# Cross-attention pair on one core: the layer norm's doubling moved into gamma, the second queries summed half by half, the scores begun on the first half of the queries

## The chip, the cores and the metric

The kernel runs on one core of a Trainium2 chip, as a single program with one instruction stream for each engine: TensorE (PE; the loading of its weights is shown as PEld), VectorE (DVE), ScalarE (ACT), GpSimd (POOL) and SyncE (SP). The metric is the device time of one launch in microseconds (us), as the median of several runs.

## What is computed

Sixteen blocks of 512 tokens with 256 features (`x`, 16 x 512 x 256) pass through two cross-attentions onto 64 context rows per block. The part of the reference that the change touches is the second one:

```python
q = gelu(einsum('bqd,dp->bqp', virtual_node, Wq) + bq)     # virtual_node is x', what the first attention gives
k = gelu(einsum('bnd,dp->bnp', node_features, Wk) + bk)
v = gelu(einsum('bnd,dp->bnp', node_features, Wv) + bv)
scores = einsum('bqp,bnp->bqn', q, k)
attended = einsum('bqn,bnp->bqp', softmax(scores), v)
x = einsum('bqp,pd->bqd', attended, Wf) + bf + virtual_node
mu = mean(x); var = mean((x - mu)^2)
return (x - mu) * rsqrt(var + 1e-5) * ln_gamma + ln_beta
```

The first attention normalises tokens and context by their root mean square, lets each token attend to the context row that its index names and to that row's two neighbours, with 16 heads and squared-relu weights, projects and adds the tokens.

## The kernel before

All of it works on features by tokens: a block is a tile of 128 partitions by 2 halves of the features (`c` or `g`, 0 and 1) by 512 tokens. The loop `steps` runs over 17 steps; step s works on five blocks at once: e = s (loading), a = s-1 (first queries and key products), f = s-2 (first attention's values), b = s-3 (first output projection, x', second queries and scores) and n = s-4 (softmax, output, layer norm, write). The last block is finished after the loop by code of its own, in halves of the tokens (names with `half_`). Every engine has its instructions in the order in which the program writes them, and semaphores (`wait_ge`, `then_inc`) tie the engines together; no planner orders anything. A product in full precision is three matmuls (`product`, L430 to L434): the high part of weight and data, low weight with high data, high weight with low data. So each operand is split in a rounded high part and a remainder.

The places that the change and the prediction speak of, within one step:

- **x' and its split.** DVE adds projection and tokens into `xpT`, second half of the features first (L1100). ACT rounds each half into `xp_hi` (L896), DVE takes the remainder `xp_lo` of each half (L1103), also second half first.
- **The second queries.** `queries1(0)` and `queries1(1)` on PE (L627 to L642) each sum six matmuls over both halves of x', c = 0 first. Ahead of `queries1(0)` PE waits until both halves of `xp_hi` and of `xp_lo` are there. Between the two stands `up_keys(a)` (L638, matmuls of L479), which writes the PSUM banks from which the layer norm reads, and so waits for `zn_ready`, which ACT raises after the last of the four scalings of block n.
- **Gelu and scores.** ACT makes `q1T` from the two results (L909) and raises `q1_ready` once, after both. PE's scores (L662) wait for that.
- **The layer norm.** PE's output matmuls of block n (L590) are followed by DVE's statistics (L1089, four instructions), ten small POOL instructions on 128 x 4 values (`norm_factors`, L351 to L372), ACT's four scalings to `zn` (L862, in two pairs with a copy of L829 between them), POOL's product with gamma (L381) and sum with beta (L383), and the write. POOL's factors: `half_rstd` is half of 1/std (L368, a power), `rstd` doubles it (L371), `nbias` is minus the mean over the std (L372), from `nmean2` (L366).
- **On POOL behind gamma and beta** stands the remainder of the next tokens, `x_lo` (L343), for which PE's first queries wait.

The functions that the diff touches follow with their line numbers.

Of the kernel before, what the change touches and what calls it, by code (L numbers as in the profile page):

```python
# [23 lines left out]
def xattn_pair(nc: bass.Bass, xT, ctx, ctxT, idx, vectors, wq0T, wk0T, wv0T, wo0T,  # L24
# [9 lines left out]
    with es:  # L34
# [3 lines left out]
        def sem(name):  # L38
            return es.enter_context(nc.semaphore(name))
# [10 lines left out]
        lnb_row = sb("lnb_row", [P, D])  # L50
        minus_half = sb("minus_half", [P, CT])
# [53 lines left out]
        def rows(t):  # L105
# [46 lines left out]
            "stats_ready", "parts_ready", "gap_ready", "mean_ready", "var_ready", "rstd_ready", "nbias_ready"))  # L152
        kvs_zero = [sem(f"kvs_zero_{r}") for r in range(2)]
# [166 lines left out]
        def _(pool):  # L320
# [30 lines left out]
            def norm_factors(n):  # L351
# [14 lines left out]
                G.tensor_scalar(nmean2[:, :], mean2[:, :], -1.0, None, ALU.mult).then_inc(mean_ready, 1)  # L366
# [4 lines left out]
                G.tensor_tensor(rstd[:, :], half_rstd[:, :], half_rstd[:, :], ALU.add).then_inc(nbias_ready, 1)  # L371
                G.tensor_tensor(nbias[:, :], nmean2[:, :], half_rstd[:, :], ALU.mult).then_inc(nbias_ready, 1)  # L372

            def scale_rows(n):

                pool.wait_ge(zn_ready, 2 * n + 2)
                if n == 0:
                    pool.wait_ge(ln_in, 16 * 2)
                else:
                    pool.wait_ge(out_done, 16 * n)  # L380
                G.tensor_tensor(zo, zn, lng_row[:, :].unsqueeze(1).broadcast_to([P, TT, D]), ALU.mult).then_inc(zg_ready, 1)  # L381
                pool.wait_ge(zg_ready, n + 1)
                G.tensor_tensor(zo, zo, lnb_row[:, :].unsqueeze(1).broadcast_to([P, TT, D]), ALU.add).then_inc(zo_ready, 1)  # L383
# [6 lines left out]
            def step(e, a, f, b, n):  # L390
                if n is not None:
                    norm_factors(n)
                    scale_rows(n)
                if e is not None:
                    split_x_lo(e)
                if n is not None:
                    write_rows(n)
# [12 lines left out]
            scale_rows(LAST - 1)  # L410
# [7 lines left out]
        def _(pe):  # L418
# [133 lines left out]
            def step(e, a, f, b, n):  # L552
# [74 lines left out]
                def queries1(i):  # L627
                    for c in range(DC):
                        product(ps[:, Q1_BANKS[i], :], *weight("q1", c, i), xp_hi[:, c, :], xp_lo[:, c, :], c == 0, c == DC - 1, q1_mm)

                if b is not None:
                    pe.wait_ge(xph_ready, 2 * b + 2)
                    pe.wait_ge(xpl_ready, 2 * b + 2)
                    queries1(0)
# [22 lines left out]
                if b is not None:  # L657
                    pe.wait_ge(q1_ready, b + 1)

                    for c in range(DC):  # L660
                        for h in range(2):
                            i = mm(ps[h * K:(h + 1) * K, 4, 0:2 * P], k1T[:, c, b * K:(b + 1) * K],  # L662
                                   q1T[:, c, 2 * h * P:(2 * h + 2) * P], start=(c == 0), stop=(c == DC - 1))
# [109 lines left out]
        def _(act):  # L773
# [81 lines left out]
            def step(e, a, f, b, n):  # L855
                def normalise(tiles):

                    act.wait_ge(nbias_ready, 2 * n + 2)
                    if n > 0:
                        act.wait_ge(zg_ready, n)  # L860
                    for j in tiles:
                        i = A(zn[:, j, :], out_rows(j), ACT.Identity,  # L862
                              bias=nbias[:, j:j + 1], scale=rstd[:, j:j + 1])
                    i.then_inc(zn_ready, 1)
# [41 lines left out]
                if b is not None:  # L906
                    for i in range(DC):
                        act.wait_ge(q1_mm, 2 * b + i + 1)
                        last = A(q1T[:, i, :], ps[:, Q1_BANKS[i], :], ACT.Gelu, bias=vec[:, 2, i:i + 1])  # L909
                    last.then_inc(q1_ready, 1)  # L910
# [344 lines left out]
```

## Time and profile before

| | us |
|---|---|
| median of 3 runs | 372.47 |
| lowest and highest run | 370.99, 372.87 |
| the profiled execution's own time | 372.61 |
| its span, first to last instruction | 370.8 |
| PE busy, DVE busy, ACT busy, POOL busy in the span | 338.5, 311.5, 246.6, 180.4 |

The profile shows one execution. Busy time is the time in which an engine has an instruction in work; idle time is given with what ended it. The page also follows the chain of work back from the last instruction, at each step to what released it. Matmuls overlap each other in the records, so that what counts on PE is the distance from one start to the next, not the duration.

### The profile page before, as it was taken

To read this page: it belongs to the slowest core of one execution; us is meant where nothing else is said; L and a number is where in the kernel's file an instruction comes from. 1 tells how busy PE (TensorE), PEld (TensorE's weight loads), DVE (VectorE), ACT (ScalarE), POOL (GpSimd) and SP (SyncE) were. 2 spreads that over 40 slices of the span, in tenths; PEclk is the share of its full clock that TensorE was granted. 3 is DMA by queue.
4 is the path that set the end of the run, shared out by engine and by line. 5 is a ranking of instruction groups with operands and counts; after the bars stand their busy time and mean duration, and the time that the engine had idled before them with its cause. 6 is when DMAs were issued, how large, how long until landed. Compare 5 with 4: busy or idle time off the path is not lost.

```text
span 370.8 us, 5551 instructions
## 1 busy us (share of the span) xinstructions
PE 338.5 (91%) x1904; PEld 238.5 (64%) x1904; DVE 311.5 (84%) x486; ACT 246.6 (66%) x491; POOL 180.4 (49%) x218
## 2 busy tenths in 40 slices
PE   3995899999999999999999999999999999986871
PEld 1571486767676767676767686858686767655740
DVE  0878588699999999999999999999989898986745
ACT  4796243275959595959595959595959595847552
POOL 3712210023838383838383737474747474626063
PEclk9997899999999999999999999999999999999995
DMA  7978211931222222323231313141414131010103
GB/s 245 319 228 236 74 57 40 216 113 54 91 103 95 98 100 91 109 85 114 75 124 60 138 60 139 60 139 59 141 57 142 57 143 57 2 57 0 58 0 113
DMA packets 21946, 38.48 MB, mean 104 GB/s; under 512 B 2144, under 2 KB 8288, under 8 KB 21920
## 3 DMA queue, kind: packets, MB, share of 16 engines
q1 hardware_dynamic: 18800, 29.48, 24.9%
q0 software_dynamic: 2160, 7.87, 6.1%
q10 hardware_dynamic: 960, 0.79, 0.7%
q8 instruction: 15, 0.25, 0.3%
q14 instruction: 11, 0.09, 0.1%
HBM read 17.29 MB, written 8.39 MB: 69 GB/s over the span
## 4 chain that ended last, share of the span: by engine, by line
PE 56%; ACT 12%; POOL 11%; DVE 11%; issue 10%; ACTq 0%; POOLq 0%
PE ps L510 8%; ACT bufs L862 6%; PE ps L432 6%; PE ps L434 6%; PE ps L433 6%; PE ps L479 5%; DVE stats L1089 5%; PE ps L662 4%; PE ps L561 4%; PE ps L671 4%; PE ps L590 4%; PE ps L485 3%; POOL rstd L371 3%; PE ps L566 2%; ACT bufs L829 2%
## 5 line engine op out<-in xcount | busy, mean ns | idle before, releaser
L343 POOL TENSOR_TENSOR x_lo<-x_ring,x_hi 128x1024 fp32r<-128x1024 f32 x16 | 38.3, 2396 | 43.7 <-ACT x_hi L825 43.7
L1020 DVE TENSOR_TENSOR qkp<-ps,bufs 128x1024 f32<-128x1024 f32 x48 | 55.9, 1214 | 0.9 <-PE ps L479 0.8
L381 POOL TENSOR_TENSOR bufs<-bufs,lng_row 128x1024 f32<-128x1024 f32 x15 | 36.0, 2403 | 37.0 <-ACT bufs L862 35.0
L896 ACT ACTIVATE xp_hi<-bufs 128x512 fp32r<-128x512 f32 x30 | 18.9, 632 | 50.6 <-DVE bufs L1100 50.6
L1031 DVE TENSOR_TENSOR ps<-ps,wn 128x1024 f32<-128x1024 f32 x32 | 39.2, 1224 | 1.2 <-PE ps L485 1.2
L355 POOL TENSOR_TENSOR mean_gap<-stats 128x4 f32<-128x4 f32 x14 | 2.8, 197 | 71.1 <-DVE stats L1089 71.1
L383 POOL TENSOR_TENSOR bufs<-bufs,lnb_row 128x1024 f32<-128x1024 f32 x15 | 35.6, 2377 | 1.2
L510 PE MATMUL ps<-qkp,cst 128*32 128x512 f32 x192 | 32.2, 624 | 1.7 <-DVE qkp L1020 1.7
L510 PE MATMUL ps<-bufs,cst 128*32 128x512 f32 x64 | 31.9, 624 | 0.0
L862 ACT ACTIVATE bufs<-ps,nbias,rstd 128x256 f32<-128x256 f32 x56 | 28.6, 569 | 3.0 <-POOL nbias L372 3.0
L432 PE MATMUL ps<-xp_hi,wh_q 128*128 128x512 f32 (+1 forms) x68 | 27.1, 398 | 2.6 <-DVE xp_lo L1103 1.9
L829 ACT ACTIVATE bufs<-ps 128x512 f32<-128x512 f32 x32 | 19.0, 597 | 14.3 <-PE ps L434 14.3
L432 PE MATMUL ps<-x_hi,wh_q 128*128 128x512 f32 x64 | 26.5, 414 | 0.0
L432 PE MATMUL ps<-o_hi,wh_o 128*128 128x512 f32 (+1 forms) x68 | 26.0, 382 | 0.3 <-DVE o_lo L1172 0.3
L434 PE MATMUL ps<-xp_lo,wh_q 128*128 128x512 f32 (+1 forms) x68 | 25.8, 380 | 0.0
L433 PE MATMUL ps<-o_hi,wl_o 128*128 128x512 f32 (+1 forms) x68 | 25.8, 379 | 0.0
L433 PE MATMUL ps<-xp_hi,wl_q 128*128 128x512 f32 (+1 forms) x68 | 25.8, 379 | 0.0
L434 PE MATMUL ps<-o_lo,wh_o 128*128 128x512 f32 (+1 forms) x68 | 25.6, 377 | 0.0
L434 PE MATMUL ps<-x_lo,wh_q 128*128 128x512 f32 x64 | 25.1, 393 | 0.0
L433 PE MATMUL ps<-x_hi,wl_q 128*128 128x512 f32 x64 | 25.1, 391 | 0.0
L909 ACT ACTIVATE bufs<-ps,vec 128x512 f32<-128x512 f32 x30 | 20.6, 689 | 5.3 <-PE ps L434 5.2
L1100 DVE TENSOR_TENSOR bufs<-ps,x_ring 128x512 f32<-128x512 f32 x30 | 20.5, 685 | 4.2 <-PE ps L434 4.1
(205 smaller groups left out, 924.4 us busy)
## 6 DMA issues: line engine op xcount, KB each, us to landing
x_ring<-xT SPq DMA_DIRECT2D x16, 512.0 KB, 3.5
out<-bufs POOLq DMA_DIRECT2D x15, 512.0 KB, 3.4
idx_ring<-idx SPq DMA_DIRECT2D x16, 256.0 KB, 4.1
kvs<-kv SPq DMA_DIRECT2D x32, 126.0 KB
wkv_lo<-kv SPq DMA_DIRECT2D x32, 126.0 KB
vfd<-bufs SPq DMA_DIRECT2D x8, 256.0 KB, 4.1
qkp<-ctxT SPq DMA_DIRECT2D x2, 512.0 KB, 7.2
bufs<-ctx SPq DMA_DIRECT2D x2, 512.0 KB, 8.5
```

The lines of the kernel that those rows point to most:

```text
L343: G.tensor_tensor(x_lo[:, :, :], x_ring[:, e % RING, :, :], f32_view(x_hi[:, :, :]), ALU.subtract).then_inc(xl_ready, 2)
L381: G.tensor_tensor(zo, zn, lng_row[:, :].unsqueeze(1).broadcast_to([P, TT, D]), ALU.mult).then_inc(zg_ready, 1)
L383: G.tensor_tensor(zo, zo, lnb_row[:, :].unsqueeze(1).broadcast_to([P, TT, D]), ALU.add).then_inc(zo_ready, 1)
L432: mm(o, hi, m_hi, start=start, stop=False)
L433: mm(o, lo, m_hi, start=False, stop=False)
L434: last = mm(o, hi, m_lo, start=False, stop=stop)
L510: i = mm(ps[32 * s:32 * s + 32, 0, :], sum_sel[:, g if s < SHIFTS else 2, :], qk[:, s, g, :] if s < SHIFTS else xsq[:, g, :], start=(g == ...
L829: A(q0[:, g, :], ps[:, Q0_BANKS[g], :], ACT.Copy).then_inc(q0_cp, 1)
L862: i = A(zn[:, j, :], out_rows(j), ACT.Identity, bias=nbias[:, j:j + 1], scale=rstd[:, j:j + 1])
L909: last = A(q1T[:, i, :], ps[:, Q1_BANKS[i], :], ACT.Gelu, bias=vec[:, 2, i:i + 1])
L1020: V.tensor_tensor(qk[:, s, :, :], ps[:, bank0:bank0 + 2, :], q0, ALU.mult).then_inc(qk_ready, 1)
L1031: V.tensor_tensor(dst.rearrange("p a (h d) -> p (a h) d", d=HD), picked(bank0).rearrange("p a (h d) -> p (a h) d", d=HD), wn[:, s, :, :].r ...
```

## The change

Three edits. First, `queries1` takes c = 1 ahead of c = 0, and the two waits for `xp_hi` and `xp_lo` are split: `queries1(0)` waits for the second half only, and for the first half when it comes to it. Second, ACT raises `q1_ready` after each gelu, and PE waits ahead of each half of the scores' sum for its own half of the queries; the halves stay in their order. Third, L371 (`rstd`) is dropped from `norm_factors`: ACT scales by `half_rstd`, `nmean2` is made with -0.5 in the place of -1.0, so that `zn` is half of what it was, and POOL multiplies by `lng_twice`, which is twice gamma and made once, at block 0. The last block's own code keeps gamma and `rstd`.

```diff
@@ -48,6 +48,7 @@
         bf_row = sb("bf_row", [P, D])
         lng_row = sb("lng_row", [P, D])
         lnb_row = sb("lnb_row", [P, D])
+        lng_twice = sb("lng_twice", [P, D])
         minus_half = sb("minus_half", [P, CT])
         x_ring = sb("x_ring", [P, RING, DC, T])
         idx_ring = sb("idx_ring", [P, RING, T], i32)
@@ -150,6 +151,7 @@
         eT_mm, eT_ready, z_mm = map(sem, ("eT_mm", "eT_ready", "z_mm"))
         stats_ready, parts_ready, gap_ready, mean_ready, var_ready, rstd_ready, nbias_ready = map(sem, (
             "stats_ready", "parts_ready", "gap_ready", "mean_ready", "var_ready", "rstd_ready", "nbias_ready"))
+        twice_ready = sem("twice_ready")
         kvs_zero = [sem(f"kvs_zero_{r}") for r in range(2)]
         kvs_in = [sem(f"kvs_in_{r}") for r in range(2)]
         zn_ready, zg_ready, zo_ready, out_done, last_zg, last_zo, last_out_done = map(sem, (
@@ -363,22 +365,23 @@
                 pool.wait_ge(var_ready, 2 * n + 1)
                 G.tensor_tensor(var4[:, :], m2_part[:, :], gap_sq[:, :], ALU.add).then_inc(var_ready, 1)
                 pool.wait_ge(mean_ready, 2 * n + 1)
-                G.tensor_scalar(nmean2[:, :], mean2[:, :], -1.0, None, ALU.mult).then_inc(mean_ready, 1)
+                G.tensor_scalar(nmean2[:, :], mean2[:, :], -0.5, None, ALU.mult).then_inc(mean_ready, 1)
                 pool.wait_ge(var_ready, 2 * n + 2)
                 G.tensor_tensor(half_rstd[:, :], var4[:, :], minus_half[:, 0:TT], ALU.pow).then_inc(rstd_ready, 1)
                 pool.wait_ge(rstd_ready, n + 1)
                 pool.wait_ge(mean_ready, 2 * n + 2)
-                G.tensor_tensor(rstd[:, :], half_rstd[:, :], half_rstd[:, :], ALU.add).then_inc(nbias_ready, 1)
                 G.tensor_tensor(nbias[:, :], nmean2[:, :], half_rstd[:, :], ALU.mult).then_inc(nbias_ready, 1)
 
-            def scale_rows(n):
+            def scale_rows(n, gamma):
 
                 pool.wait_ge(zn_ready, 2 * n + 2)
                 if n == 0:
                     pool.wait_ge(ln_in, 16 * 2)
+                    G.tensor_tensor(lng_twice[:, :], lng_row[:, :], lng_row[:, :], ALU.add).then_inc(twice_ready, 1)
+                    pool.wait_ge(twice_ready, 1)
                 else:
                     pool.wait_ge(out_done, 16 * n)
-                G.tensor_tensor(zo, zn, lng_row[:, :].unsqueeze(1).broadcast_to([P, TT, D]), ALU.mult).then_inc(zg_ready, 1)
+                G.tensor_tensor(zo, zn, gamma[:, :].unsqueeze(1).broadcast_to([P, TT, D]), ALU.mult).then_inc(zg_ready, 1)
                 pool.wait_ge(zg_ready, n + 1)
                 G.tensor_tensor(zo, zo, lnb_row[:, :].unsqueeze(1).broadcast_to([P, TT, D]), ALU.add).then_inc(zo_ready, 1)
 
@@ -390,7 +393,7 @@
             def step(e, a, f, b, n):
                 if n is not None:
                     norm_factors(n)
-                    scale_rows(n)
+                    scale_rows(n, lng_twice)
                 if e is not None:
                     split_x_lo(e)
                 if n is not None:
@@ -407,7 +410,7 @@
                 G.tensor_tensor(nbias[:, cols], mean2[:, cols], rstd[:, cols], ALU.mult).then_inc(half_nbias, 1)
 
             norm_scales(0, slice(0, TT))
-            scale_rows(LAST - 1)
+            scale_rows(LAST - 1, lng_row)
             norm_scales(1, slice(0, 2))
             norm_scales(2, slice(2, TT))
             write_rows(LAST - 1)
@@ -625,12 +628,14 @@
                     centre_keys(a)
 
                 def queries1(i):
-                    for c in range(DC):
-                        product(ps[:, Q1_BANKS[i], :], *weight("q1", c, i), xp_hi[:, c, :], xp_lo[:, c, :], c == 0, c == DC - 1, q1_mm)
+
+                    for c in (1, 0):
+                        if i == 0:
+                            pe.wait_ge(xph_ready, 2 * b + (2 - c))
+                            pe.wait_ge(xpl_ready, 2 * b + (2 - c))
+                        product(ps[:, Q1_BANKS[i], :], *weight("q1", c, i), xp_hi[:, c, :], xp_lo[:, c, :], c == 1, c == 0, q1_mm)
 
                 if b is not None:
-                    pe.wait_ge(xph_ready, 2 * b + 2)
-                    pe.wait_ge(xpl_ready, 2 * b + 2)
                     queries1(0)
                 if a is not None:
                     if n is not None:
@@ -655,9 +660,8 @@
                 if f == 0:
                     final_values(1)
                 if b is not None:
-                    pe.wait_ge(q1_ready, b + 1)
-
                     for c in range(DC):
+                        pe.wait_ge(q1_ready, 2 * b + c + 1)
                         for h in range(2):
                             i = mm(ps[h * K:(h + 1) * K, 4, 0:2 * P], k1T[:, c, b * K:(b + 1) * K],
                                    q1T[:, c, 2 * h * P:(2 * h + 2) * P], start=(c == 0), stop=(c == DC - 1))
@@ -855,12 +859,12 @@
             def step(e, a, f, b, n):
                 def normalise(tiles):
 
-                    act.wait_ge(nbias_ready, 2 * n + 2)
+                    act.wait_ge(nbias_ready, n + 1)
                     if n > 0:
                         act.wait_ge(zg_ready, n)
                     for j in tiles:
                         i = A(zn[:, j, :], out_rows(j), ACT.Identity,
-                              bias=nbias[:, j:j + 1], scale=rstd[:, j:j + 1])
+                              bias=nbias[:, j:j + 1], scale=half_rstd[:, j:j + 1])
                     i.then_inc(zn_ready, 1)
 
                 if n is not None:
@@ -906,8 +910,7 @@
                 if b is not None:
                     for i in range(DC):
                         act.wait_ge(q1_mm, 2 * b + i + 1)
-                        last = A(q1T[:, i, :], ps[:, Q1_BANKS[i], :], ACT.Gelu, bias=vec[:, 2, i:i + 1])
-                    last.then_inc(q1_ready, 1)
+                        A(q1T[:, i, :], ps[:, Q1_BANKS[i], :], ACT.Gelu, bias=vec[:, 2, i:i + 1]).then_inc(q1_ready, 1)
                 if e is not None:
                     split_x_hi(e)
                 if b is not None:
```

What it does to the instructions of POOL in `norm_factors`. Before (from the variance, in every step with a block n; at block 0 here):

```order
L366 TENSOR_SCALAR nmean<-mean 128x4 [waits mean_ready]
L368 TENSOR_TENSOR half_rstd<-var,minus_half 128x4 [waits var_ready]
L371 TENSOR_TENSOR rstd<-half_rstd 128x4 [waits mean_ready,rstd_ready]
L372 TENSOR_TENSOR nbias<-nmean,half_rstd 128x4
L381 TENSOR_TENSOR bufs<-bufs,lng_row 128x1024 [waits ln_in,zn_ready]
L383 TENSOR_TENSOR bufs<-bufs,lnb_row 128x1024 [waits zg_ready]
```

Of the change, at the same place:

```order
L368 TENSOR_SCALAR nmean<-mean 128x4 [waits mean_ready]
L370 TENSOR_TENSOR half_rstd<-var,minus_half 128x4 [waits var_ready]
L373 TENSOR_TENSOR nbias<-nmean,half_rstd 128x4 [waits mean_ready,rstd_ready]
L380 TENSOR_TENSOR lng_twice<-lng_row 128x256 [waits ln_in,zn_ready]
L384 TENSOR_TENSOR bufs<-bufs,lng_twice 128x1024 [waits twice_ready]
L386 TENSOR_TENSOR bufs<-bufs,lnb_row 128x1024 [waits zg_ready]
```

One instruction is gone and `nbias` stands in its place, with its waits; the doubling of gamma is there at block 0 alone.

PE at the end of the loop, step 17, where no block a is left: the second queries up to the back-transposes of x' (L671 before, L675 now). Before:

```order
L432 MATMUL ps<-xp_hi,wh_q 128x512
L433 MATMUL ps<-xp_hi,wl_q 128x512
L434 MATMUL ps<-xp_lo,wh_q 128x512
L485 MATMUL ps<-kv,onehot 128x256 [waits xp_ready]
L485 MATMUL ps<-kv,onehot 128x256 x3
L662 MATMUL ps<-bufs,k1T 64x256 [waits q1_ready]
L662 MATMUL ps<-bufs,k1T 64x256 x3
L671 MATMUL ps<-cst,bufs 128x128 [waits zn_ready]
```

Of the change:

```order
L435 MATMUL ps<-xp_hi,wh_q 128x512 [waits xpl_ready,xph_ready,att_ready]
L436 MATMUL ps<-xp_hi,wl_q 128x512
L437 MATMUL ps<-xp_lo,wh_q 128x512
L435 MATMUL ps<-xp_hi,wh_q 128x512 [waits xpl_ready,xph_ready]
...
L488 MATMUL ps<-kv,onehot 128x256 [waits xp_ready]
L488 MATMUL ps<-kv,onehot 128x256 x3
L666 MATMUL ps<-bufs,k1T 64x256 [waits q1_ready]
L666 MATMUL ps<-bufs,k1T 64x256
L666 MATMUL ps<-bufs,k1T 64x256 [waits q1_ready]
L666 MATMUL ps<-bufs,k1T 64x256
L675 MATMUL ps<-cst,bufs 128x128 [waits zn_ready]
```

The matmuls are the same in number and size; a second pair of waits stands in the middle of the first queries' sum and a second wait in the middle of the scores' sum.

## Rows read from the trace of the kernel before

**Rows 1.** The page: busy time, its share of the span and the instructions of each engine

```profile
PE 338.5 (91%) x1904; PEld 238.5 (64%) x1904; DVE 311.5 (84%) x486; ACT 246.6 (66%) x491; POOL 180.4 (49%) x218
```

**Rows 2.** The chain of waits from 195 to 240 us, one block: start, us, what

```profile
202.32 0.75 POOL rstd L371
...
205.73 0.74 PE ps L479 x2
...
224.48 0.73 PE ps L479 x2
```

**Rows 3.** L371's duration (ns, min/median/max), and one of the waits

```profile
L371 POOL TENSOR_TENSOR rstd<-half_rstd x14: 200/747/757, 89.9 to 333.3; 128x4 f32<-128x4 f32 x14
...
ACT bufs L862 <- POOL nbias L372: 3.0, 13, 0.8
```

**Rows 4.** Timeline, 202.2 to 203.3 us: start, duration, engine, line, operation, [idle before]

```profile
202.32 0.75 POOL L371 TENSOR_TENSOR rstd<-half_rstd 128x4 f32<-128x4 f32 x1
202.32 1.47 DVE L1103 TENSOR_TENSOR xp_lo<-bufs,xp_hi 128x512 fp32r<-128x512 f32 x2
202.44 0.63 ACT L896 ACTIVATE xp_hi<-bufs 128x512 fp32r<-128x512 f32 x1 [0.32 <-DVE bufs L1100]
...
203.02 0.20 POOL L372 TENSOR_TENSOR nbias<-nmean,half_rstd 128x4 f32<-128x4 f32 x1
...
203.25 0.56 ACT L862 ACTIVATE bufs<-ps,nbias,rstd 128x256 f32<-128x256 f32 x1 [0.18 <-POOL nbias L372]
```

**Rows 5.** Timeline of block 0, 89.8 to 90.7 us

```profile
89.86 0.20 POOL L371 TENSOR_TENSOR rstd<-half_rstd 128x4 f32<-128x4 f32 x1
...
90.01 0.65 POOL L372 TENSOR_TENSOR nbias<-nmean,half_rstd 128x4 f32<-128x4 f32 x1
```

**Rows 6.** Timeline of PE from 203.3 to 206.3 us

```profile
203.38 0.61 PE L479 MATMUL ps<-onehot,kv 128*128 128x512 f32 x2
203.94 0.47 PE L432 MATMUL ps<-xp_hi,wh_q 128*128 128x512 f32 x1
...
205.18 0.40 PE L434 MATMUL ps<-xp_lo,wh_q 128*128 128x512 f32 x1
```

**Rows 7.** Timeline of PE, ACT and DVE, 207.4 to 211.2 us

```profile
207.68 0.62 PE L479 MATMUL ps<-onehot,wkv_lo 128*128 128x512 f32 x2
...
207.88 0.69 ACT L909 ACTIVATE bufs<-ps,vec 128x512 f32<-128x512 f32 x1 [0.21 <-PE ps L434]
...
208.14 0.63 PE L485 MATMUL ps<-kv,onehot 128*128 128x256 f32 x4
...
208.70 1.08 PE L662 MATMUL ps<-bufs,k1T 128*64 128x256 f32 x8
...
211.06 0.42 DVE L1129 TENSOR_REDUCE nmax<-ps 128x4 f32<-128x256 f32 x1 [0.33 <-PE ps L675]
```

**Rows 8.** Timeline of POOL, block 0, and of PE where it needs x_lo

```profile
98.02 2.38 POOL L343 TENSOR_TENSOR x_lo<-x_ring,x_hi 128x1024 fp32r<-128x1024 f32 x1
...
101.75 0.47 PE L432 MATMUL ps<-x_hi,wh_q 128*128 128x512 f32 x1
```

**Rows 9.** Timeline of step 17, the last of the loop, 332 to 341.5 us

```profile
333.35 0.59 POOL L371 TENSOR_TENSOR rstd<-half_rstd 128x4 f32<-128x4 f32 x1
333.89 0.65 POOL L372 TENSOR_TENSOR nbias<-nmean,half_rstd 128x4 f32<-128x4 f32 x1
...
334.57 1.94 ACT L862 ACTIVATE bufs<-ps,nbias,rstd 128x256 f32<-128x256 f32 x4 [0.82 <-POOL nbias L372]
...
337.82 1.27 ACT L909 ACTIVATE bufs<-ps,vec 128x512 f32<-128x512 f32 x2
...
339.14 1.08 PE L662 MATMUL ps<-bufs,k1T 128*64 128x256 f32 x8 [1.06 <-ACT bufs L909]
```

**Rows 10.** Stretches: us, busy PE, PEld, DVE, ACT, POOL, granted clock, DMA

```profile
345.00:353.00 8.00, 7.32 (x57) 6.41 (x56) 4.88 (x15) 3.74 (x6) 1.03 (x1) 1.00 0.01 2
...
361.00:363.00 2.00, 1.62 (x5) 0.70 (x3) 1.77 (x9) 0.00 (x0) 0.38 (x1) 0.50 0.00 0
```

## The prediction, made before the changed kernel ran

> **What bounds the kernel now.** I read the page first: PE has work in 91% of the span, DVE in 84% [rows 1]. So no engine is free to take much, and the question for each edit is which wait ends last where it acts. The chain of waits answers for the middle of the run [rows 2]. It repeats every 18.75 us (205.73 to 224.48), and always in the same way: PE's output matmuls of block n, DVE's statistics, POOL's small instructions, ACT's scalings, and PE's `up_keys` (L479), which must not write the banks before the last scaling has read them. From there PE runs through to the next output matmuls. So the layer norm of block n is on the path, and the POOL instruction that the change drops, L371, is a link of it with 0.75 us. The durations come from one execution with 372.61 us of its own; the median of the runs is 372.47, so 0.14 comes off the sum at the end.
>
> **The layer norm's doubling.** L371 takes 0.75 us in nearly every block, at least 0.20 [rows 3]. At block 6 it starts at 202.32 with DVE's first remainder (L1103) and ends at 203.07; L372 ends at 203.22 and ACT starts scaling at 203.25, after 0.18 of idle time [rows 4]. Block 0 shows what the 0.75 is: there L371 came through in 0.20 just ahead of L1103, and L372 took 0.65 in its place [rows 5]. Two instructions of the same kind and size; whichever stands beside DVE's first remainder is held until that is over. L371 has no work worth 0.75, and `nbias`, which moves into its place, will be held in the same way. Were the 0.75 work, `nbias` would end so early that ACT alone set the start, 0.28 sooner in each block, and the sum would be that of rival 1. The Trainium skill, "SBUF — State Buffer", section "Who interferes with whom", speaks against this part of the change: a VectorE instruction with two SBUF inputs, as L1103 is, and a GpSimd one that reads SBUF exclude each other for the whole instruction, and the first to issue wins. The rows of blocks 0 and 6 agree: a held instruction ends when the first remainder does.
>
> So `nbias` will end at 203.07 instead of 203.22: 0.15 earlier. ACT can take it: its previous instruction (L896) ends at 202.44 + 0.63 = 203.07, and back to back ACT overlaps two such instructions by 0.10 (four scalings of 0.56 in 1.94, rows 9). ACT's idle time before scaling adds up to 3.0 us over 13 blocks, 0.8 of it at the last [rows 3]: 2.2 over 12, 0.18 each, so the twelve blocks are alike. **12 x 0.15 = 1.8 us.** Block 0 had next to no idle time there; between 0.03 and 0.16, I take 0.1. The bounds for each of the twelve are 0 (something else holds `up_keys`) and 0.18 + 0.10 = 0.28 (`nbias` is early and ACT itself is the limit).
>
> Do the others follow a step that is 0.15 shorter? PE has 0.32 to spare ahead of `up_keys`: its last query matmul started at 205.18, they follow one another every 0.23, and L479 started at 205.73 [rows 2, 6]. DVE idles 0.33 before the maxima of the scores, for PE [rows 7], and everything else before them on DVE is further ahead of its users. So both have slack for 0.15, and DVE would be the next bound at 0.33.
>
> **The second queries' order.** `queries1(0)` now waits for both halves of the remainder: it starts at 203.94 instead of 203.38 + 2 x 0.23 = 203.84 [rows 6], 0.15 after L1103's second half (203.79, rows 4). With c = 1 first it need not wait, which gives back 0.10 and some 0.09 of a slower first matmul. But behind it stands `up_keys`, where PE already has 0.32 too many, and the gain lies in that wait. I take 0 in the twelve blocks; if the wait there went away it would be worth 0.19. Step 3, which has no layer norm, could gain those 0.19 once; I leave them out. An order of 1, 0 costs nothing in itself: the same six matmuls. POOL's, SP's and ACT's queues are not reordered.
>
> **The scores' first half.** In the middle of the run PE reaches L662 at 208.70, 0.13 after the second gelu's end at 208.57 [rows 7]. In step 17, where PE really stood waiting for gelu, it started 0.05 after its end (337.82 + 1.27 = 339.09, rows 9). So in the middle PE does not wait, and the term is 0; at most 0.08 a block. The added waits, when already satisfied, cost nothing: L485 at 208.14 has one ahead of it and follows the second matmul of L479 (207.68 + 0.23 = 207.91) after the usual 0.23 [rows 7]. The upper end for one is the 0.19 of a wait that does stop PE.
>
> **Gamma doubled at block 0.** One POOL instruction of 128 x 256, about a quarter of L381's or L343's 2.4 us: 0.6 once. POOL's `x_lo` would end near 98.02 + 2.38 + 0.6 = 101.0, PE asks for it at 101.75 [rows 8]. Hidden; if that 0.75 were gone it would cost 0.6 once.
>
> **The end of the loop.** Step 17 has no block a and is bound otherwise: POOL, four scalings, a table load, two gelus, scores, each waiting for the one before [rows 9]. Here L372 was held by the second remainder too, and ACT idled 0.82 before scaling. Without L371 `nbias` is done when the first remainder is, at 333.35 + 0.59 = 333.94 instead of 334.54: 0.60 off. Then the first gelu ends near 337.9 and the second at 338.49, and PE sums the first half in between. The second half starts at 338.54 and takes half of 1.08, so the scores end at 339.1 to 339.2 instead of 340.22. PE is there in time: its queries can start on the first remainder too, 0.6 earlier. **1.05 us**, with bounds of 0.6 (the split brings nothing) and 1.4 (`nbias` is not held). What follows, the maxima and the last block's own code, waits for these scores and moves with them.
>
> **Sum:** 1.8 + 0.1 + 1.05 = 2.95; 372.61 - 2.95 = 369.66, and against the median 369.5.
>
> **Rivals.** (1) `nbias` slips through. In the middle blocks L371 and L1103 start at the same hundredth; at block 0 0.02 decided the other way. By the stamps POOL is not behind DVE there, so a shift of 0.02 could let `nbias` (0.20) through in every block. (The Trainium skill's "SBUF — State Buffer", section "Who interferes with whom", gives the lock to the first to issue, which by these stamps would be POOL.) Then ACT is the limit: 12 x 0.28 + 0.1 + 1.4 = 4.9, which gives 367.6. Against it: the stamps were as good as equal in all those blocks too, and POOL lost. Chance 0.17. (2) The middle gains nothing, because a wait that I read as slack takes the place of `nbias` (DVE before the maxima is the nearest, 0.33), or the blocks' gain is lost again on PE's added waits; only the end brings 1.05: 371.4. Chance 0.17. (3) Slower: PE's clock. It was granted in full up to 361 and at half, 1.2 GHz, behind it [rows 10], after PE had stood waiting for the softmax of the last block. The change moves the waits of the end against that grant. If it fell before 345, the 7.3 us of PE's busy time in the stretch to 353 would double, and the last block's code is a chain in which little else could cover it: up to 369.5 + 7.3 = 376.8. It decides if the grant is 0.50 anywhere in 341 to 353. Against it: PE stood still there before as well, and kept its clock. Chance 0.05. That the edit does not do what it says is part of the forecast: `nbias` inherits the stall, and the new order of the queries is hidden.
>
> **Chances and range.** The forecast has 0.56, (1) 0.17, (2) 0.17, (3) 0.05, and 0.05 is left for the rest. A measurement here can tell about 0.5% from no change, 1.86 us, so faster means below 370.6. The forecast and (1) are there, 0.73, and a little of the rest; (2) with most of the rest makes no change, 0.21; slower 0.05. The range takes in (1) and (2) with the runs' own scatter of some tenths: 367.4 to 371.6.
>
> **What would show it.** After the change: the distance from one `up_keys` to the next at 18.60 instead of 18.75; `nbias` with a duration near 0.75 and ACT's idle time before scaling near zero; PE's wait before the first second-query matmul gone and its wait for the scaling still there, longer by some 0.04; L662 in the middle no closer to the matmul before it; in step 17 the scores in two parts and the end of them 1.05 earlier against the statistics of that step. `nbias` at 0.20 and a distance of 18.47 would show (1); 18.75 again would show (2) and make me wrong, as would a step 17 that gains less than 0.6.

## The result, and the profile after

| | before | after |
|---|---|---|
| median of 11 runs each, us | 372.28 | 369.13 |
| lowest and highest | 370.54, 372.87 | 366.17, 370.94 |
| ratio, with its 95% interval | | 0.9932 [0.9909, 0.9955] |
| the profiled execution's own time, us | 372.61 | 369.03 |
| its span, us | 370.8 | 367.2 |

The kernel became faster by 0.7%, or 3.15 us between the medians; 2.95 were forecast (369.5). The interval of the ratio reaches from 0.45% to 0.91% faster. So a gain is clear of the noise, and the 0.5% that the prediction took as the least that a measurement can tell lies inside it: more than 0.5% is likely, not certain.

Block 6 of the changed kernel, its timeline where the rows of before are [rows 4, 6]: start, duration, engine, line, operation, and in brackets idle time and what ended it. L373 was L372, L1106 was L1103, L900 was L896, L866 was L862, L435 and L482 were L432 and L479.

```profile
200.63 1.48 DVE L1106 TENSOR_TENSOR xp_lo<-bufs,xp_hi 128x512 fp32r<-128x512 f32 x2
200.63 0.74 POOL L373 TENSOR_TENSOR nbias<-nmean,half_rstd 128x4 f32<-128x4 f32 x1
200.75 0.63 ACT L900 ACTIVATE xp_hi<-bufs 128x512 fp32r<-128x512 f32 x1 [0.32 <-DVE bufs L1103]
201.41 0.56 ACT L866 ACTIVATE bufs<-ps,nbias,half_rstd 128x256 f32<-128x256 f32 x1
201.68 0.61 PE L482 MATMUL ps<-onehot,kv 128*128 128x512 f32 x2
202.13 0.39 PE L435 MATMUL ps<-xp_hi,wh_q 128*128 128x512 f32 x1
203.27 0.39 PE L437 MATMUL ps<-xp_lo,wh_q 128*128 128x512 f32 x1
203.88 0.50 PE L482 MATMUL ps<-onehot,wkv_lo 128*128 128x512 f32 x1 [0.23 <-ACT bufs L866]
```

In this block, as in most, `nbias` has taken L371's place beside DVE's first remainder, and L371's duration. ACT now scales right after its rounding of x' ends (200.75 + 0.63 = 201.38). The second queries start 0.23 after the matmul before them (201.68 + 0.23 + 0.23 = 202.14, and the row has 202.13), without a wait, and PE waits as before at `up_keys`: 203.88 - 203.27 - 0.23 = 0.38, where it was 0.32.

The chain of waits of the changed kernel, from one block to the next (start, us, what), answers to [rows 2]:

```profile
200.63 0.75 POOL nbias L373
201.41 0.49 ACT bufs L866
...
203.88 0.73 PE ps L482 x2
...
222.48 0.73 PE ps L482 x2
```

The distance is 222.48 - 203.88 = 18.60; before it was 18.75. The duration of `nbias` over its 14 calls (ns: min, median, max) answers to [rows 3]:

```profile
L373 POOL TENSOR_TENSOR nbias<-nmean,half_rstd x14: 201/743/758, 89.2 to 330.6; 128x4 f32<-128x4 f32 x14
```

and from the list of waits (us in total, times, longest):

```profile
ACT bufs L866 <- POOL nbias L373: 0.2, 1, 0.2
```

ACT's idle time before scaling fell from 3.0 us to 0.2, and what is left is in step 17. That step's timeline, which answers to [rows 9]:

```profile
330.60 0.59 POOL L373 TENSOR_TENSOR nbias<-nmean,half_rstd 128x4 f32<-128x4 f32 x1
331.22 1.94 ACT L866 ACTIVATE bufs<-ps,nbias,half_rstd 128x256 f32<-128x256 f32 x4 [0.22 <-POOL nbias L373]
334.47 1.27 ACT L913 ACTIVATE bufs<-ps,vec 128x512 f32<-128x512 f32 x2
335.21 1.23 PE L666 MATMUL ps<-bufs,k1T 128*64 128x256 f32 x8 [0.48 <-ACT bufs L913]
```

The scores (L666) begin before the second gelu has ended (334.47 + 1.27 = 335.74), and end at 335.21 + 1.23 = 336.44. Counted from the start of the first remainder of x' in this step (330.44) that is 6.00; before it was 340.22 - 333.18 = 7.04.

**Where the 3.6 us between the two profiled executions went**, by the starts of fixed instructions in the two traces: the first maxima of the scores (L1129), the statistics of blocks 0, 12 and 13 (L1089), the last maxima in the loop, and as the last mark the end of DVE's last instruction.

| stretch | before | after | difference |
|---|---|---|---|
| start to the first maxima | 79.92 | 79.31 | -0.61 |
| to the statistics of block 0 | 5.94 | 5.84 | -0.10 |
| to those of block 12, twelve blocks | 224.95 | 223.05 | -1.90 |
| to those of block 13 | 18.55 | 18.40 | -0.15 |
| to the last maxima, the end of step 17 | 12.15 | 11.12 | -1.03 |
| to the end | 26.50 | 26.69 | +0.19 |

The first and the last row are not the change's doing. The stretch from 36 to 40 us (columns as in [rows 10]; the number before the DMA share is the granted clock) reads, before:

```profile
36.00:40.00 4.00, 2.91 (x16) 0.59 (x16) 3.97 (x3) 0.59 (x1) 2.36 (x1) 0.50 0.60 172
```

and after:

```profile
36.00:40.00 4.00, 2.57 (x19) 0.63 (x17) 3.28 (x3) 1.68 (x3) 2.02 (x1) 0.99 0.61 172
...
357.00:359.00 2.00, 2.00 (x6) 1.11 (x4) 1.42 (x8) 0.00 (x0) 0.00 (x0) 0.50 0.00 0
```

PE had half its clock there in the one execution and its whole clock in the other, before anything that the change touches has run. All thirteen profiled executions of this case, whatever the edit, agree on what this costs, by the mean granted clock from 30 to 44 us and the time up to the first maxima: at 1.00 it is 76.7 to 77.5 us (four executions), at 0.88 78.8 to 79.3 (four, the changed kernel among them), at 0.76 79.9 to 80.0 (three, the kernel before among them), at 0.63 81.5 (two). At the end the half clock met a few more of the last matmuls than before.

### The profile page after: what moved, and what is told of

It is laid out like the page before. It is cut to its first block, busy times and chain, and to the rows that moved or that the text cites. A ratio compares the mean times of both kernels' runs of the same rounds, so it can differ in the third digit from the quotient of the medians.

```text
span 367.2 us, 5553 instructions
## 1 busy us (share of the span) xinstructions
PE 336.1 (92%) x1904; PEld 240.3 (65%) x1904; DVE 311.3 (85%) x486; ACT 246.5 (67%) x491; POOL 177.9 (48%) x205
## 4 chain that ended last, share of the span: by engine, by line
PE 55%; ACT 11%; issue 11%; DVE 11%; POOL 11%; ACTq 0%; POOLq 0%
PE ps L513 8%; PE ps L435 6%; ACT bufs L866 6%; PE ps L437 5%; PE ps L436 5%; DVE stats L1092 5%; PE ps L482 5%; PE ps L666 4%; PE ps L564 4%; PE ps L675 4%; PE ps L593 4%; PE ps L488 3%; POOL nbias L373 3%; ACT bufs L833 2%; PE ps L569 2%
## 5 line engine op out<-in xcount | busy, mean ns | idle before, releaser
L900 ACT ACTIVATE xp_hi<-bufs 128x512 fp32r<-128x512 f32 x30 | 19.0, 633 | 50.6 <-DVE bufs L1103 50.6
L384 POOL TENSOR_TENSOR bufs<-bufs,lng_twice 128x1024 f32<-128x1024 f32 x14 | 33.7, 2407 | 32.5 <-ACT bufs L866 32.5
L513 PE MATMUL ps<-qkp,cst 128*32 128x512 f32 x192 | 30.7, 598 | 1.7 <-DVE qkp L1023 1.7
L513 PE MATMUL ps<-bufs,cst 128*32 128x512 f32 x64 | 30.5, 598 | 0.0
L866 ACT ACTIVATE bufs<-ps,nbias,half_rstd 128x256 f32<-128x256 f32 x56 | 28.6, 568 | 0.6 <-POOL nbias L373 0.2
L435 PE MATMUL ps<-xp_hi,wh_q 128*128 128x512 f32 (+1 forms) x68 | 26.0, 382 | 2.0 <-DVE xp_lo L1106 1.3
L435 PE MATMUL ps<-x_hi,wh_q 128*128 128x512 f32 x64 | 26.5, 413 | 0.0
L435 PE MATMUL ps<-o_hi,wh_o 128*128 128x512 f32 (+1 forms) x68 | 26.0, 382 | 0.3 <-DVE o_lo L1175 0.3
L1103 DVE TENSOR_TENSOR bufs<-ps,x_ring 128x512 f32<-128x512 f32 x30 | 20.5, 685 | 4.2 <-PE ps L437 4.1
```

The lines of the kernel that those rows point to most:

```text
L384: G.tensor_tensor(zo, zn, gamma[:, :].unsqueeze(1).broadcast_to([P, TT, D]), ALU.mult).then_inc(zg_ready, 1)
L435: mm(o, hi, m_hi, start=start, stop=False)
L513: i = mm(ps[32 * s:32 * s + 32, 0, :], sum_sel[:, g if s < SHIFTS else 2, :], qk[:, s, g, :] if s < SHIFTS else xsq[:, g, :], start=(g == ...
L866: i = A(zn[:, j, :], out_rows(j), ACT.Identity, bias=nbias[:, j:j + 1], scale=half_rstd[:, j:j + 1])
```

## The experiments

Times are ratios to the kernel before, run on the same chip in the same job. "Distance" is the mean over the twelve intervals between the statistics of blocks 0 and 12 in the profiled execution, 18.75 before and 18.59 for the changed kernel by this measure. `one_sum`, `copy_behind` and `copy_old_order` ran 4 times, `both`, `no_scores` and `filled_end` 6 times, the others 10 or 12 times, so that the times of the first six say less than their traces.

### One part at a time

`norm_only`, against the changed kernel (the second queries and the scores as before):

```diff
-                    for c in (1, 0):
-                        if i == 0:
-                            pe.wait_ge(xph_ready, 2 * b + (2 - c))
-                            pe.wait_ge(xpl_ready, 2 * b + (2 - c))
+                    for c in range(DC):
...
+                    pe.wait_ge(xph_ready, 2 * b + 2)
+                    pe.wait_ge(xpl_ready, 2 * b + 2)
...
-                        pe.wait_ge(q1_ready, 2 * b + c + 1)
+                    pe.wait_ge(q1_ready, b + 1)
```

> The dropped L371 and the doubled gamma alone, with the queries in their old order and one signal for both gelus. My theory: all of the gain in the middle of the run comes from here, so one up_keys follows the other after 18.60 us instead of 18.75, as in the changed kernel; step 17 gains 0.60 for the earlier nbias but not the split scores' 0.45; about 2.5 us in all, 369.8. Rival (the queries' order is needed, because PE would otherwise be late at up_keys): the distance stays above 18.65.

Measured: ratio 0.9931 [0.9899, 0.9963], median 369.53. Distance 18.61. The layer norm's edit alone brings what the whole change brings in the middle; the rival is out. The profiled execution was the slowest of the twelve runs (372.99), but it had the full clock from 36 to 332 us, where the distance is read. Two neighbours in this execution, the last query matmul and `up_keys`:

```profile
203.65 0.40 PE L437 MATMUL ps<-xp_lo,wh_q 128*128 128x512 f32 x1
204.06 0.74 PE L482 MATMUL ps<-onehot,wkv_lo 128*128 128x512 f32 x2
```

PE's spare time there is 0.41 - 0.23 = 0.18, so even with the old order PE was not late. The 0.60 in step 17 can't be read from this execution: the step took 12.98, more than before, because PE's granted clock fell in it (the number before the DMA share):

```profile
331.00:337.00 6.00, 4.88 (x16) 3.92 (x16) 3.34 (x4) 4.43 (x8) 3.87 (x3) 0.72 0.00 0
```

The experiment `no_scores` below, at full clock there, has the step at 11.54, 0.61 less than before.

`order_only`, against the kernel before:

```diff
-                    for c in range(DC):
-                        product(ps[:, Q1_BANKS[i], :], *weight("q1", c, i), xp_hi[:, c, :], xp_lo[:, c, :], c == 0, c == DC - 1, q1_mm)
+                    for c in (1, 0):
+                        if i == 0:
+                            pe.wait_ge(xph_ready, 2 * b + (2 - c))
+                            pe.wait_ge(xpl_ready, 2 * b + (2 - c))
+                        product(ps[:, Q1_BANKS[i], :], *weight("q1", c, i), xp_hi[:, c, :], xp_lo[:, c, :], c == 1, c == 0, q1_mm)
...
-                    pe.wait_ge(xph_ready, 2 * b + 2)
-                    pe.wait_ge(xpl_ready, 2 * b + 2)
```

> The second queries' order and its split waits alone. My theory: PE starts them 0.10 to 0.19 earlier in every block and waits as much longer for the scaling, so the distance from up_keys to up_keys stays 18.75; step 3 gains 0.1; in step 17 PE is earlier but then waits for gelu, nothing gained; total within 0.2 us of the kernel before. Rival: each block gains its 0.19, 18.56, 2.3 us in all.

Measured: 0.999 [0.9955, 1.0026]; distance 18.75. From the timeline of PE:

```profile
205.26 0.39 PE L432 MATMUL ps<-xp_hi,wh_q 128*128 128x512 f32 x1
...
206.39 0.39 PE L434 MATMUL ps<-xp_lo,wh_q 128*128 128x512 f32 x1
207.16 0.50 PE L479 MATMUL ps<-onehot,wkv_lo 128*128 128x512 f32 x1 [0.37 <-ACT bufs L864]
```

The spare time is 0.77 - 0.23 = 0.54: 0.32 and the 0.2 that PE gained and then waited. Up to the statistics of block 0 it takes 5.84 instead of 5.94: the 0.10 of the table above is this edit's, in step 3.

`scores_only`, against the kernel before:

```diff
-                    pe.wait_ge(q1_ready, b + 1)
-
                     for c in range(DC):
+                        pe.wait_ge(q1_ready, 2 * b + c + 1)
...
-                        last = A(q1T[:, i, :], ps[:, Q1_BANKS[i], :], ACT.Gelu, bias=vec[:, 2, i:i + 1])
-                    last.then_inc(q1_ready, 1)
+                        A(q1T[:, i, :], ps[:, Q1_BANKS[i], :], ACT.Gelu, bias=vec[:, 2, i:i + 1]).then_inc(q1_ready, 1)
```

> The split signal of gelu and the split wait of the scores alone. My theory: nothing in the middle (18.75, and L662 follows the matmul before it after 0.21 as before), 0.45 us once in step 17, so 0.4 us less than before in all. Rival (PE does wait for the second gelu in every block, 0.08): 18.67 and 1.4 us in all. Rival (a satisfied wait inside a sum costs a restart): the distance grows by 0.05 to 0.19 a block.

Measured: 1.0058 [1.0024, 1.0092], median 373.31: slower than before. Of what was written down ahead only the last rival, a restart after each satisfied wait, would make it slower, and it is out: the distance did not grow (18.74). Step 17 gained 0.44 (11.71 instead of 12.15). What the profiled execution lost lies behind, 28.58 instead of 26.50 from the last maxima to the end, and there the granted clock says why:

```profile
345.00:353.00 8.00, 7.32 (x50) 6.38 (x49) 4.68 (x14) 3.35 (x6) 0.68 (x1) 0.87 0.00 0
```

In the kernel before that stretch had 1.00 [rows 10]. The runs agree. Each run comes with its mean granted clock, and over the 61 runs (of 63) of the kernel before that three jobs' comparisons used, the time follows it. The changed kernel's column has the runs of the result, which are from another job:

| mean granted clock | before, us | changed kernel, us | scores_only, us |
|---|---|---|---|
| 0.985 to 0.987 | 368.8 to 371.0 | 366.2, 367.5 | none |
| 0.980 to 0.983 | 370.3 to 372.0 | 368.9 to 369.4 | 371.3 to 371.7 |
| 0.976 to 0.978 | 372.3 to 373.6 | 369.7 to 370.1 | 372.1 to 373.6 |
| 0.973, 0.974 | 373.8 to 374.0 | 370.9 | none |
| 0.967 to 0.971 | none | none | 374.4 to 375.5 |

At the same clock `scores_only` is as fast as before; four of its ten runs had a clock below that of all 61. The 0.44 of step 17 can't be seen in these times.

### Is it step 17's split that costs the clock?

`scores_middle`, against `scores_only`:

```diff
-                        pe.wait_ge(q1_ready, 2 * b + c + 1)
+                        pe.wait_ge(q1_ready, 2 * b + (2 if a is None else c + 1))
```

> The kernel before with the split signal of gelu, and PE waiting half by half in all steps but 17, where it waits for both as before. If step 17's split causes the lower clocks of scores_only, the granted clocks are here those of the kernel before (0.974 to 0.987) and the time is 371.4, the same as before. If the split in the middle blocks or chance was the cause, the time is again 1 to 2 us above before.

Measured: 0.9993 [0.9969, 1.0017], median 371.85; clocks 0.978 to 0.987 in 12 runs; distance 18.74. So the split in the middle is worth nothing and costs nothing. The low clocks of `scores_only` went away with the split of step 17. But that split is not the only way to them: the profiled execution of `scores_middle`, too, had a stretch at half clock in step 17 and took 13.00 for it, and `norm_only`, which has no split at all and ran on the same chip as `scores_only`, had 0.971 to 0.973 in four of its twelve runs. `scores_middle` ran on another chip, so the chip stays a rival too. That step 17's split causes the low clocks is not shown.

`no_scores`, the changed kernel with the signal and the wait of before (the diff of `scores_only` the other way round):

> The changed kernel with one signal for both gelus and one wait of the scores, as before. My theory: middle distance 18.60; in step 17 the gain is 0.60 and not 1.04, so it is 0.45 us slower than the changed kernel at the same granted clock. Rival, after scores_only came out slower than the kernel before: the earlier first half of the scores in step 17 spreads PE's work so that the grant falls more often in the end; then the runs here have higher clocks than those of scores_only and the median is not above that of the changed kernel.

Measured: 0.9918 [0.9889, 0.9948], median 368.55, clocks 0.977 to 0.985. The trace has 11.54 in step 17 where the changed kernel has 11.12: the split is worth 0.42 there, as worked out. The times do not show it, and both signs of the rival came: higher clocks than in `scores_only`, and a median not above that of the changed kernel. At 0.985 these runs took 367.6 to 368.1, at 0.980 and 0.981 369.0, as the changed kernel. So within the whole change the split of the scores has no gain that these runs can tell. That the split lowers the clock is not shown by this: in the changed kernel, which has it, the clocks were 0.973 to 0.986 in 11 runs. Why four runs of `scores_only` were lower still is open; ten runs may also simply have drawn badly.

This execution shows one thing more. In two of its blocks, 9 and 11, `nbias` was not held; the row of block 9:

```profile
257.20 0.20 POOL L373 TENSOR_TENSOR nbias<-nmean,half_rstd 128x4 f32<-128x4 f32 x1
```

The next statistics came after 18.44 and 18.46 there, against 18.59 to 18.61 where it was held up to block 8. So rival 1 of the prediction can happen, block by block, with the changed kernel's layer norm. How often it does in runs without a trace isn't recorded, and it may hide some of the 0.42.

### What holds `nbias`?

`pool_later`, against the changed kernel (the tile `spare` is new and read by nothing):

```diff
                 G.tensor_scalar(nmean2[:, :], mean2[:, :], -0.5, None, ALU.mult).then_inc(mean_ready, 1)
+                G.tensor_tensor(spare[:, :], mean_e, mean_o, ALU.subtract)
```

> The changed kernel with one idle small instruction more on POOL, ahead of the power; its result is used by nothing. It makes nbias start 0.16 to 0.20 later, when DVE's first remainder has begun. If nbias is held by that remainder (my theory), it still ends when the remainder ends, its duration falls from 0.75 to about 0.58, and the distance stays at 18.60. If its 0.75 is its own time (what follows a power is slow), it stays at 0.75 and the distance grows to 18.76 or more, 2 us in all.

Measured: 0.9938 [0.9908, 0.9968], median 369.06. Distance 18.59, unchanged. The timeline of block 6 and the durations (ns) of all `nbias`:

```profile
198.85 1.47 DVE L1108 TENSOR_TENSOR xp_lo<-bufs,xp_hi 128x512 fp32r<-128x512 f32 x2
...
199.00 0.59 POOL L375 TENSOR_TENSOR nbias<-nmean,half_rstd 128x4 f32<-128x4 f32 x1
199.63 0.56 ACT L868 ACTIVATE bufs<-ps,nbias,half_rstd 128x256 f32<-128x256 f32 x1
```

```profile
L375 POOL TENSOR_TENSOR nbias<-nmean,half_rstd x14: 379/592/611, 87.5 to 328.9; 128x4 f32<-128x4 f32 x14
```

The instruction starts 0.15 after the remainder, takes 0.15 less, and ends where it ended. POOL did one instruction more in each block for nothing, and no time was lost.

`one_sum`, against the changed kernel (`sums` is a tile of 128 x 4 x 2, whose two parts the next instructions read):

```diff
-                G.tensor_tensor(m2_sum[:, :], m2_e, m2_o, ALU.add).then_inc(parts_ready, 1)
+                G.tensor_tensor(sums[:, :, :], stats[:, :, 1:3], stats[:, :, 4:6], ALU.add).then_inc(parts_ready, 1)
...
-                G.tensor_tensor(mean2[:, :], mean_e, mean_o, ALU.add).then_inc(mean_ready, 1)
```

> The changed kernel with one small POOL instruction less ahead of the power: the sums of the means and of the squares are made in one instruction over both. nbias can start 0.15 earlier, before DVE's first remainder. My theory (it is held only when it meets the remainder): its duration falls from 0.75 to 0.20, it ends 0.7 earlier, ACT becomes the limit and starts scaling 0.13 earlier, 18.47 from up_keys to up_keys, 1.6 us less than the changed kernel. If the 0.75 is its own time, the duration stays 0.75 and it ends 0.15 earlier.

Measured: 0.9895 [0.9839, 0.9951], median 367.32. Distance 18.46, 0.29 less than before, where the prediction had 0.28 as the bound at which ACT is the limit. Block 6:

```profile
200.40 0.20 POOL L372 TENSOR_TENSOR nbias<-nmean,half_rstd 128x4 f32<-128x4 f32 x1
200.47 1.48 DVE L1105 TENSOR_TENSOR xp_lo<-bufs,xp_hi 128x512 fp32r<-128x512 f32 x2
200.59 0.63 ACT L899 ACTIVATE xp_hi<-bufs 128x512 fp32r<-128x512 f32 x1 [0.32 <-DVE bufs L1102]
201.13 0.55 ACT L865 ACTIVATE bufs<-ps,nbias,half_rstd 128x256 f32<-128x256 f32 x1
```

0.07 ahead of DVE, `nbias` takes 0.20. ACT starts scaling 0.09 before its rounding ends (200.59 + 0.63 = 201.22), which is its own limit. The power stands ahead of `nbias` here too, so a slowness after a power is excluded.

All thirteen traces, with these two among them, tell the same. In each take the fourteen small instructions that come first behind the power (`rstd` or `nbias`), 182 in all. 53 passed in 0.20 and 129 were held. Each that passed had its start stamped at least 0.017 us ahead of the first remainder's; each that was held had a lead of 0.016 or less, or none. And whatever was held, L372 in block 0 and step 17 of the kernel before too, ended 0.055 to 0.063 after the end of the remainder beside it.

### What bounds the middle next?

`copy_behind`, against the changed kernel, on ACT:

```diff
-                    copy_q0(a, 1)
                 if n is not None:
                     normalise(range(0, 2))
+                if a is not None and f is not None:
+                    copy_q0(a, 1)
```

> The changed kernel with ACT's copy of the first queries' second half behind all four scalings instead of between the two pairs. The last scaling ends 0.45 earlier. PE's spare time ahead of up_keys is 0.39, so PE could gain 0.39; DVE's spare time before the maxima of the scores, 0.33 to 0.41 before and 0.15 less now, is the nearer limit. I expect 18.35 to 18.40 from up_keys to up_keys, 2.4 to 3.0 us less than the changed kernel, with DVE's wait before the maxima gone. Rival (the copy is late for DVE's key products): DVE waits ahead of L1023 and the distance is 18.50 or more.

Measured: 0.9817 [0.9751, 0.9883], median 363.36. Distance 18.16, 0.2 better than I had as the limit. Between 100 and 300 us the list of waits (us in total, times, longest) has no wait of PE at `up_keys`, and none of DVE for the maxima:

```profile
PEld ps L564 <- DVE qkp L1062: 9.8, 11, 0.9
...
DVE bufs L1104 <- PE ps L437: 2.7, 11, 0.3
DVE rsum L1065 <- ACT ps L873: 2.5, 11, 0.2
```

Here PE itself ran from the queries through `up_keys` without a wait, and not only there. From 120 to 280 us it is busy all the time (columns as in [rows 10]), where the kernel before has 158.73 of 160:

```profile
120.00:280.00 160.00, 160.00 (x972) 116.73 (x971) 151.34 (x228) 122.21 (x248) 97.79 (x117) 1.00 0.30 101
```

So the limit is PE's own work at 18.16, and not DVE: its 0.33 before the maxima did not stop the step at 18.35.

This kernel also repeats the race of block 0 at a finer grain: in the same run, `nbias` and the first remainder of two blocks, POOL's row and then DVE's:

```profile
214.19 0.75 POOL L373 TENSOR_TENSOR nbias<-nmean,half_rstd 128x4 f32<-128x4 f32 x1
...
214.20 0.68 DVE L1107 TENSOR_TENSOR xp_lo<-bufs,xp_hi 128x512 fp32r<-128x512 f32 x1
...
286.82 0.20 POOL L373 TENSOR_TENSOR nbias<-nmean,half_rstd 128x4 f32<-128x4 f32 x1
...
286.83 0.72 DVE L1107 TENSOR_TENSOR xp_lo<-bufs,xp_hi 128x512 fp32r<-128x512 f32 x1
```

The stamps differ by 0.014 and by 0.018 us before rounding. In the first POOL is held, in the second it is not: on either side of the line between 0.016 and 0.017.

`copy_old_order`: `copy_behind` with the second queries as before (the diff of `order_only` the other way round).

> The kernel copy_behind (ACT's copy behind all four scalings) with the second queries in their old order and both waits ahead of them. There PE no longer waits at up_keys, so the order's gain is no longer hidden: without it the distance should grow by up to 0.19, from 18.16 to 18.30 or 18.35, 1.7 to 2.3 us in all. If the order is worth nothing even so, 18.16.

Measured: 0.9834 [0.9792, 0.9876], median 365.24. Distance 18.31 against 18.16: the order is worth 0.15 a block once PE does not wait at `up_keys`.

`both`: `one_sum` and `copy_behind` together.

> Both of these edits. If DVE is the limit that I read, the two do not add: 18.34 to 18.38, at most 0.5 us less than the copy's move alone. If DVE is not the limit, they add up to 18.22.

Measured: 0.9788 [0.9736, 0.984], median 363.43; distance 18.17. They do not add: PE is the limit here too, and an earlier `nbias` brings nothing more.

`filled_end`, against `both`:

```diff
             half_back(1)
+            pe.wait_ge(zn_ready, 2 * LAST)
+            for _ in range(4):
+                mm(ps[:, 6, :], w_hi["q1"][:, 0, 0:P], xp_hi[:, 0, :], start=True, stop=True)
             half_transposed(0)
```

> The kernel both with four matmuls more at the end, on operands that are there, into a bank that is no longer read; they fill 0.9 of the 1.3 us in which PE waits for the last block's softmax, and their result is used by nothing. If the granted clock falls ahead of the last output matmuls because PE stood still there, it falls later or not at all and the end from the last maxima of the loop to the last store shortens by up to 0.5 us; if the grant does not depend on it, nothing changes or the four matmuls cost 0.1.

Measured: 0.9766 [0.9732, 0.98], median 362.79, the fastest version here: 2.3% below the kernel before. Its runs had clocks of 0.980 to 0.991, those of `both` 0.973 to 0.990. But in the two profiled executions the end took 26.50 either way, as the half clock came after the last output matmuls in both. Inconclusive: the intervals overlap, and no trace shows the fall being put off.

## Why the prediction was right

- **The doubling.** Its step stands, in size and in cause. Forecast: `nbias` inherits the stall, 0.15 for each of twelve blocks and 0.1 for block 0, 1.9 together. Measured: 2.05 for the thirteen (1.90 and 0.15 in the table). `norm_only` shows that it is this edit; `pool_later` and `one_sum` show that the 0.75 is the time until the remainder is over. The twelve blocks have 1.89 of it, 0.16 each where 0.15 were forecast. At block 0 the forecast has the size nearly right and the cause wrong: `nbias` was not held there (0.20, 89.15 us), which is rival 1, and the block gained 0.16 (18.47 after 18.63) instead of 0.1. In `norm_only`, where it was held at block 0 (0.76), that block gained 0.04. In the profiled execution of the changed kernel rival 1 did not happen in any other block, but it is near: in `no_scores` it came in two blocks, and with 0.07 more lead (`one_sum`) it holds in every block of the middle.
- **The queries' order.** Forecast 0 in the middle, because of the wait at `up_keys`, and 0.19 if that wait went away. `order_only` has 0; `copy_old_order` has 0.15 without the wait. Step 3, which the prediction named and left out of the sum, gave 0.10.
- **The scores' halves.** Forecast 0 in the middle: `scores_middle` has 18.74. In step 17, 0.45 of the 1.05; the traces have 0.42 to 0.44. But as a saving in run time it does not appear.
- **Gamma at block 0.** It took 0.61 on POOL, and `x_lo` was still there 0.69 before PE asked. Hidden.
- **Step 17.** 1.05 forecast, 1.03 measured.
- **Where I was off.** The next bound: I had DVE's 0.33 before the maxima as the nearest limit, and the middle could shrink by 0.59 in all (18.75 to 18.16). It did not touch this forecast, which needed 0.15. And the clock: the prediction says that it was granted in full up to 361 in the kernel before, which is a misreading, as the stretch from 36 to 40 us at 0.50 above shows. I had it as a rare rival with one fall near 345. It is rather a scatter over the runs, at a price of 0.8 to 2.1 us a stretch and not 7.3, since no fall seen lasted through 345 to 353. The medians agree with the forecast to 0.4 us, which is closer than the interval of 0.9 us either way, so that the last tenths are luck; the profiled pair moved by 3.6, of which 0.4 is the net of the two ends, where the clock differed.

## What to carry to other kernels

Before booking a small instruction's duration as a gain, look at what the neighbouring engine does in the same moment: if its duration ends with the other's instruction, removing it hands the wait to the next one. Starting later did not help here (`pool_later`); only starting clearly ahead of the other did (`one_sum`). An edit ahead of a wait that remains is worth nothing until that wait is gone; here the same reordering gave 0 and then 0.15 a block. Compare runs at equal granted clock when the effect is under 1%: stretches at half clock at the start and the end move this kernel by up to as much as the change does or more (81.5 against 76.7 us up to the first maxima).

## What the runs showed that I had not expected

- POOL's small instruction is held although its start is stamped up to 0.016 us before DVE's, and passes from 0.017 on, without an exception in 182 cases. So which of two close stamps comes first does not tell who is held, but the size of the lead does: a shift of two hundredths of a microsecond can be worth 0.15 us a block here.
- The time of one and the same kernel follows its mean granted clock: from 0.987 to 0.974, 370 to 374 us. The Trainium skill, "TensorE: Matmul & The Clock Gate", section "What's actually happening", gives an idle engine the half clock. The traces agree as far as the stretches at half clock seen here lie behind or among PE's waits, at the start (between 31.6 and 42.1 us) and in and behind step 17. But the same wait does not always bring a fall: PE stood still from 30.2 to 32.2 us in the kernel before and in `pool_later`, and the clock fell at 33.3 in the one and stayed full in the other.
- What a split gains that starts some matmuls earlier can be lost in the clock's scatter: in `scores_only` step 17 became 0.44 shorter and the rest of the end 2.1 longer in the profiled execution, at a clock that fell in it. Whether the split had a part in that fall is not shown.
